# One semaphore for both tanh parts, fewer waits of VectorE on itself, its loop turned elsewhere, the last stage reordered

## The reference

```
def derivative(q, p, drive):                      # q, p: 8 x 1024
    dq = q - q**3/3 - p + drive + tanh(q) @ coupling.T + bias
    dp = EPSILON * (q + ALPHA - BETA*p)
# RK4: dq1..dq4 at q, q+DT/2*dq1, q+DT/2*dq2, q+DT*dq3; p alike
q = clip(q + DT/6*(dq1+2*dq2+2*dq3+dq4), -20, 20); p = clip(p + ..., -20, 20)
x[:, t, :] += q
```

## Time and profile before

| | us |
|---|---|
| median of 3 runs | 5836.68 |
| the profiled execution | 5833.99 |
| its span | 5832.2 |
| VectorE busy | 5405.9 (93%) |
| TensorE busy | 4466.0 (77%) |
| ScalarE busy | 2597.8 (45%) |
| granted TensorE clock, mean share of full speed | 0.995 |

### The profile page before, as it was taken

The page is one execution under the profiler, slowest core; times in us unless marked ns, Lnnn a source line. Parts: engine busy times, 40 slices in busy tenths (PEclk is TensorE's granted clock), DMA queues, the critical chain, the costliest instruction groups (busy, mean ns, idle before and its releaser), DMA issues.

```text
span 5832.2 us, 592464 instructions
## 1 busy us (share of the span) xinstructions
PE 4466.0 (77%) x263627; PEld 3814.6 (65%) x263627; DVE 5405.9 (93%) x31566; ACT 2597.8 (45%) x12040; POOL 5.7 (0%) x16
## 2 busy tenths in 40 slices
PE   7887777777777777777777777777777777777777
PEld 3446666666666666666666666666666666666666
DVE  5569999999999999999999999999999999999999
ACT  3334444444444444444444444444444444444444
POOL 0000000000000000000000000000000000000000
PEclk9999999999999999999999999999999999999999
DMA  5100000000000000000000000000000000000000
GB/s 214 46 16 0 0 7 0 7 0 7 0 0 7 0 7 0 7 0 0 7 0 7 0 7 0 0 7 0 7 0 7 0 0 7 0 7 0 7 0 7
DMA packets 11597, 57.06 MB, mean 10 GB/s; under 512 B 2616, under 2 KB 2616, under 8 KB 8512
## 3 DMA queue, kind: packets, MB, share of 16 engines
q1 hardware_dynamic: 11056, 55.84, 2.4%
q10 hardware_dynamic: 528, 1.05, 0.1%
HBM read 40.11 MB, written 16.78 MB: 10 GB/s over the span
## 4 chain that ended last, share of the span: by engine, by line
DVE 48%; PE 33%; issue 16%; ACT 1%; DMA 1%; DVEq 0%; SPq 0%; ACTq 0%
PE ps L633 29%; DVE xb L675 24%; DVE xb L835 10%; DVE tanh_parts L675 6%; DVE xb L858 2%; DVE xb L950 2%; DVE xb L959 2%; PE ps L522 1%; ACT xb L446 1%; PE ps L577 1%; PE ps L540 1%; PE ps L556 1%; PE ps L566 1%; DVE drive L675 1%; DVE xb L964 1%
## 5 line engine op out<-in xcount | busy, mean ns | idle before, releaser
L633 PE MATMUL ps<-coup,tanh_parts 128*16 128x96 f16 (+1 forms) x262272 | 4120.1, 219 | 1286.1 <-DVE tanh_parts L675 1271.8
L633 PEld LDWEIGHTS ps<-coup,tanh_parts 128*16 128x16 f16 x262272 | 3654.6, 89 | 1752.3 <-issue 933.0
L675 DVE SCALAR_TENSOR_TENSOR xb<-xb 128x64 f32<-128x64 f32 (+2 forms) x17412 | 2998.8, 209 | 17.6
L446 ACT ACTIVATE xb<-xb 128x24 f32<-128x24 f32 (+1 forms) x4098 | 940.0, 229 | 2758.7 <-DVE xb L675 2747.9
L835 DVE STREAM_TRANSPOSE xb<-ps 128x96 f32<-128x96 f32 (+1 forms) x4096 | 1291.3, 315 | 198.0 <-PE ps L633 67.5
L675 DVE SCALAR_TENSOR_TENSOR tanh_parts<-xb,tanh_parts 128x24 f16<-128x24 f32 (+1 forms) x4098 | 697.9, 170 | 32.1
L495 ACT ACTIVATE xb<-xb 128x64 f32<-128x64 f32 x2048 | 500.2, 244 | 109.3 <-DVE xb L964 109.3
L452 ACT ACTIVATE tanh_parts<-xb 128x24 f16<-128x24 f32 (+1 forms) x2050 | 470.5, 230 | 64.5
L858 DVE SCALAR_TENSOR_TENSOR xb<-xb 128x64 f32<-128x64 f32 x2049 | 452.9, 221 | 0.0
L464 ACT ACTIVATE tanh_parts<-xb 128x24 f16<-128x24 f32 (+1 forms) x2048 | 356.6, 221 | 32.2
L458 ACT ACTIVATE xb<-xb 128x64 f32<-128x64 f32 x1024 | 263.5, 257 | 0.0
(11 more groups left out here) (69 smaller groups left out, 712.6 us busy)
## 6 DMA issues: line engine op xcount, KB each, us to landing
xb<-in_x SPq DMA_DIRECT2D x8, 2048.0 KB, 8.0
drive<-in_x_pt SPq DMA_DIRECT2D x8, 2048.0 KB, 25.0
out_pt<-drive SPq DMA_DIRECT2D x16, 1024.0 KB, 4.5
drive<-in_coupling_t SPq DMA_DIRECT2D x8, 512.0 KB, 11.8
mask_v<-in_cond SPq DMA_DIRECT2D x8, 132.0 KB
probs<-in_wo ACTq DMA_DIRECT2D x1, 1024.0 KB, 6.2
w_qkv<-in_wq SPq DMA_DIRECT2D x1, 64.0 KB, 4.4
w_qkv<-in_wk SPq DMA_DIRECT2D x1, 64.0 KB, 5.3
```

The source lines that it names most:

```text
L446: nc.scalar.activation(cols(tanh_sb, CHUNKS[j]), cols(q, CHUNKS[j]), ACT.Tanh, scale=unit_of[1.0])\
L633: last = nc.tensor.matmul(product(s, j)[SQ * g:SQ * g + ROWS, :], tanh_parts[:, s % 2, k, :], coup[:, k, part, g, n0:n1, :].rearrange("p c ...
L675: return V.scalar_tensor_tensor(out=out, in0=a, scalar=factor, in1=c, op0=ALU.mult, op1=op1)
```

## The change

**Semaphores.** `first_ready` and `rest_ready` of a chunk become one, `parts_ready`, which ScalarE and VectorE both raise; TensorE waits for 2 per stage, once, where it waited for each. `base_ready`, `z_rest_ready`, `p_ready`, `drive_p_ready` go; `z_ready` and `side_ready` are raised once per stage by the instruction that makes z (or y, a sum, p) and waited for at most once. In `z_of_first` of stage 3 the wait on the drive is replaced by one on `square_ready`, which ScalarE raises when it has squared the clipped q.

**Order of stage 3.** `look_ahead` goes from right behind T0 to between `cubic_of` and `base_of`; `p_next` takes its place; `clip_p` goes from behind q of chunk 1 to ahead of T1; `drive_less_p` and `clip_q` change places. In stage 2 `trace` and `p_sum_q3` change places, with a wait on `q_next` for the latter.

**The loop.** `stage` is cut in two behind the REST of chunk 1, and the loop of VectorE turns there, in stage 0, rather than behind `base_of`.

```diff
-                            pe.wait_ge(first_ready[kj], now)
-                            pe.wait_ge(rest_ready[kj], now)
+                            pe.wait_ge(parts_ready[kj], parts)
...
             def q_of(s, j, now):
-                if j == 0:
-                    dve.wait_ge(base_ready, now)
                 dve.wait_ge(product_turned[j], now)
...
                 if s == 3:
-                    look_ahead(now_at, (now + 2 * STAGES) * (COLS // STAGES))
+                    p_next()
                 q_of(s, 0, now)
...
                 if s == 3:
-                    p_next()
+                    clip_p(now)
                 turn_product(s, 1, now)
                 rest_of(parity, 0, made)
                 q_of(s, 1, now)
...
                 if s == 2:
                     z_without_last(now)
-                    trace((now - 3) * (COLS // STAGES))
+                    p_sum_q3(made)
                 if s == 3:
-                    clip_p()
+                    drive_less_p(1 - now_at)
                     clip_q(made)
-                    drive_less_p(1 - now_at, now)
                 rest_of(parity, 1, made)
+                return made
+
+            def after_rest(s, now_at, made):
...
                     cubic_of(3, made)
-                    p_sum_q3()
+                    trace((made - 4) * (COLS // STAGES))
                     base_of(3, made)
                 if s == 3:
-                    z_of_first(now).then_inc(z_ready, STAGES)
+                    dve.wait_ge(square_ready, made)
+                    z_of_first()
                     g0_of()
-                    dve.wait_ge(z_ready, now)
-                    with_first_part(0, z_first_part, z)
+                    with_first_part(0, z_first_part, z, made)
                     cubic_of(0, made)
+                    look_ahead(now_at, (made - 1 + 2 * STAGES) * (COLS // STAGES))
                     base_of(0, made)
...
-            stage(0, 0, 1)
+            made = until_rest(0, 0, 1)
             with dve.Fori(2, 2 + STAGES * (STEPS - UNROLLED), STAGES * UNROLLED) as now:
-                for s, now_at in order:
+                after_rest(0, 0, now)
+                for s, now_at in between:
                     now = stage(s, now_at, now)
+                until_rest(0, 0, now)
```

More of the change, by code:

```diff
@@ L260, in build @@
         tanh_ready = [sem(f"tanh_ready{j}") for j in range(NCH)]
-        first_ready = [sem(f"first_ready{j}") for j in range(NCH)]
-        rest_ready = [sem(f"rest_ready{j}") for j in range(NCH)]
+        parts_ready = [sem(f"parts_ready{j}") for j in range(NCH)]
         start_ready = sem("start_ready")
@@ L646, in _ @@
             last.then_inc(start_done, 1)
-            with pe.Fori(1, 1 + STAGES * STEPS, PE_STAGES) as now:
+            with pe.Fori(PARTS, PARTS * (1 + STAGES * STEPS), PARTS * PE_STAGES) as parts:
                 for s in range(PE_STAGES):
@@ L663, in _ @@
                         if place == len(ORDER) // 2:
-                            after = pe.snap(now + 1)
-                    now = after
+                            after = pe.snap(parts + PARTS)
+                    parts = after
         @block.vector
@@ L851, in rest_of @@
                 axpy(tanh_part(parity, j, REST), by_block(tanh_sb, CHUNKS[j]), TANH_SCALE,
-                     tanh_part(1 - parity, j, FIRST), ALU.subtract).then_inc(rest_ready[j], 1)
+                     tanh_part(1 - parity, j, FIRST), ALU.subtract).then_inc(parts_ready[j], 1)
             def cubic_of(stage, made):
@@ L864, in base_of, with with_first_part, z_of_first @@
                 dve.wait_ge(cubic_ready, made)
-                axpy(base[:, :], cubic[:, :], -STEP[stage] / 3 if stage < 3 else CURVE, z_first_part[:, :]).then_inc(base_ready, 1)
-            def with_first_part(stage, out, z_of_stage):
+                axpy(base[:, :], cubic[:, :], -STEP[stage] / 3 if stage < 3 else CURVE, z_first_part[:, :])
+            def with_first_part(stage, out, z_of_stage, made):
+                dve.wait_ge(z_ready, made)
                 return axpy(all_blocks(out), first_sums(), STEP[stage], all_blocks(z_of_stage))
[L871 to L875, removed]
+            def z_of_first():
+                return axpy(z[:, :], drive_p[:, :], DT / 2, q_st[0][:, :]).then_inc(z_ready, 1)
             def z_of_second():
-                axpy(z2[:, :], g0[:, :], -DT / 2 * RISE, z[:, :])
+                axpy(z2[:, :], g0[:, :], -DT / 2 * RISE, z[:, :]).then_inc(z_ready, 1)
             def y_of():
-                axpy(y[:, :], drive_p[:, :], DT, q_st[0][:, :])
+                axpy(y[:, :], drive_p[:, :], DT, q_st[0][:, :]).then_inc(side_ready, 1)
             def y_less_g0():
@@ L888, in z_of_third @@
             def z_of_third():
-                axpy(z3[:, :], rise[:, :], -DT * RISE * G1[1], y_less[:, :])
+                axpy(z3[:, :], rise[:, :], -DT * RISE * G1[1], y_less[:, :]).then_inc(z_ready, 1)
             def rise_of_first():
@@ L933, in p_sum_g0 @@
             def p_sum_g0():
-                axpy(p_sum[0][:, :], g0[:, :], P_SUM[0] / P_ALL, q_st[0][:, :], ALU.subtract)
+                axpy(p_sum[0][:, :], g0[:, :], P_SUM[0] / P_ALL, q_st[0][:, :], ALU.subtract)\
+                 .then_inc(side_ready, 1)
             def p_sum_r1():
@@ L941, in p_sum_q2, with p_sum_q3, clip_p, drive_less_p @@
                 axpy(p_sum[2][:, :], q_st[2][:, :], P_SUM[2] / P_ALL, p_sum[1][:, :])
-            def p_sum_q3():
+            def p_sum_q3(made):
+                dve.wait_ge(q_next[NCH - 1], made)
                 axpy(p_sum[3][:, :], q_st[3][:, :], 1 / P_ALL, p_sum[2][:, :])
             def p_next():
[L947 to L951, removed]
+                axpy(p_raw[:, :], p_sum[3][:, :], DT / 6 * EPS * P_ALL, p_st[:, :]).then_inc(side_ready, 1)
+            def clip_p(now):
+                dve.wait_ge(side_ready, now)
+                V.tensor_scalar(p_st[:, :], p_raw[:, :], bounds[:, 2:3], bounds[:, 3:4], ALU.max, ALU.min)
             def look_ahead(into, at):
                 axpy(drive_b[into][:, :], drive_cols[:, bass.ds(at, COLS)], inv_unit[:, 0:1], bias_b[:, :])
[L957 to L960, removed]
+            def drive_less_p(now_at):
+                V.tensor_tensor(drive_p[:, :], drive_b[now_at][:, :], p_st[:, :], ALU.subtract)
             def clip_q(made):
@@ L983, in _, with until_rest @@
             last.then_inc(start_turned, 1)
+            dve.wait_ge(start_turned, 1)
+            with_first_part(0, z_first_part, z, 1).then_inc(setup, 1)
             dve.wait_ge(setup, 10)
-            dve.wait_ge(start_turned, 1)
-            with_first_part(0, z_first_part, z).then_inc(setup, 1)
-            dve.wait_ge(setup, 11)
             base_of(0, 1)
             g0_of()
-            def stage(s, now_at, now):
+            def until_rest(s, now_at, now):
                 following = (s + 1) % STAGES
@@ L1038, in stage @@
                 if s == 1:
-                    with_first_part(2, z_first_part, z3)
+                    with_first_part(2, z_first_part, z3, made)
                     cubic_of(2, made)
```

36 lines of the change are left out of this document (17 added, 19 removed).

## The result

The changed kernel takes 5695.42 us (median of 4 runs, 5694.53 to 5696.95) against 5836.88 of the kernel before (4 runs): a ratio of 0.9758, 95% interval 0.9741 to 0.9775. The forecast was 5762, with a range from 5715 to 5812.

The account below looks back on a forecast made before the run. Bound: a circle from TensorE to VectorE and back, neither engine alone. Two stages each at 2.51, 2.55, 2.74, one at 2.55 and one at 2.63 make 20.78 us against 21.07: 74 us less, 5762 us, range 5715 to 5812.

Parts of the forecast that it names:

- The circles: TensorE-VectorE loop, T1 (transpose of chunk 1) to T1: chunk 0 2.50 us; chunk 1 2.51 in stage 1, 2.55 in 0, 2.
- One semaphore per chunk: TensorE's first load after REST: gap 0.12 to 0.05 us, the gain cut to 0.06 and 0.02 by chunk 1.
- T0 to T1: VectorE's time between the two transposes: 0.62 to 0.58 us with q earlier, counting in stage 3 and at the turn.
- Stage 3: TensorE's 0.19 us stall goes, but z waits for the square until +1.27; stage from 2.76 to 2.74 us.
- rival C: In stage 3 the wait for the square doesn't bind: stage 2.55 us, 97 us less, 5665 us; chance 0.05.
- The look ahead: Between cubic and base in stage 3: holds VectorE 0.20 us, so base comes 0.34 after cubic.
- The turn: VectorE's loop turn behind REST of chunk 1: costs the same 0.48 us, not hidden; its stage 2.68 to 2.63 us.
- A: TensorE's merged wait gains nothing, the 0.12 us stays: 28 us gained in all, 5809 us; chance 0.15.
- B: VectorE's removed waits buy nothing, transpose to transpose stays 0.62 us: 31 us, 5793 us; chance 0.07.
- D: VectorE's loop turn costs more in its new place: at 0.68 us, 13 us slower, 5849 us; chance 0.07.

## Why the prediction was right in kind and wrong in size

**The circles.** Right: but for stage 3 and the turn, which VectorE sets, each stage is set by the way from T1 through REST or FIRST to TensorE and back, and chunk 1 is late next. Stages 0 and 2 stay 0.03 to 0.04 longer than stage 1, as forecast. In stage 2 the reason is the forecast one, FIRST of chunk 1 ends last. In stage 0 behind a stage 3 FIRST of chunk 0 is late as well: the first load comes 0.51 after T1 (3010.14 to 3010.65; 0.47 in stage 2) and waits for ScalarE, which the prediction didn't have. The two ways come out within 0.01 there, so the length was right partly by luck.

**One semaphore per chunk: the term that was mis-sized.** I took the gap from REST's end to the first load, 0.12 to 0.05, and kept 1.37 from load to T1, a number read where the load stood behind a separate wait. That number held 0.02 to 0.03 of the separate wait's cost as well: with one wait the first matmul starts with the load, not 0.03 behind it. Where TensorE stands still for chunk 1 and sets T1, in stage 3 of the kernel with the clips as before, 1.34 pass from load to T1 with one wait. The stages came out 0.02 to 0.03 shorter than forecast, five of them 0.12 a turn, 31 us. My bounds for this term (0.03 and 0.12) covered only the gap to the load, so they left the other part out of the range.

**T0 to T1: the other term.** I took 0.04 from 0.62 for the separate wait, from the 0.38 at which q of chunk 0 starts behind T0 and an axpy spacing of 0.14, read among axpys in a row. The 0.38 is a row of stage 3, where the look ahead stood between T0 and q and no axpy, and the first axpy behind T0 makes way sooner than 0.14: its successor starts 0.11 after it. In the changed kernel q starts 0.31 behind T0, the three between take 0.43, and T1 comes 0.54 or 0.55 behind T0. The wait was worth 0.07 to 0.08 and not 0.04. That is 0.03 to 0.04 in three stages a turn; by the table stage 3 and the turn are 0.11 a turn under the forecast, 29 us, with 0.01 from the chain of stage 3 in it. This term had no bounds at all. The two make 60 of the 67 us; I put the rest to rounding to 0.01 and the spread of the runs.

**Stage 3.** Right to 0.05: the stall of TensorE goes, and the wait for the square holds z at +1.27 as before. What the prediction did not say is that VectorE's own chain is as long as it was: the look ahead adds 0.08 to it and the shorter T0 to T1 takes 0.07 to 0.08 away, so stage 3 is 2.694 with the new order and 2.690 with the merge alone. The 0.07 under the old 2.764 is what TensorE's stall stood above that chain, and the merge alone gives it too. That the removal of the wait for the square sets TensorE free again (rival C's size, 97 us) was measured as 98.

**The look ahead.** Right: it holds VectorE 0.20 and lengthens the chain; base is 0.08 later and stage 3 0.07 longer, twice a turn.

**The turn.** Right: moved, not hidden. The stage is 0.02 under its forecast 2.63 by T0 to T1.

**Rivals.** A is refuted by the merge alone (the words give it six stages at 2.57, its sum of 20.96 has the right five), B by the wait for base put back, C by the 512 waits for the square and a stage 3 of 2.69, D by the 0.49 at the turn and by the loop of double length. C's price is that of the next change to this kernel.

## What to carry to other kernels

Where an engine waits for two things, ask which comes last and whether it has an instruction of its own: one semaphore for both takes 0.09 us from such a wait here, 0.05 to 0.09 from most stages of a chain of 2048, and that is 122 of the 141 us; the later one on the working instruction, with both kept, gave 55. When a stall is removed, look at what the same edit makes wait: here the time that the new order of stage 3 freed went into its new wait for ScalarE, and the look ahead took what the shorter T0 to T1 gave; 100 us more lay in waiting for the clip instead. A duration read behind a wait carries a part of that wait with it; give each such term its own bounds.

## What the runs showed of the hardware

A separate waiting instruction of TensorE costs more than the delay of the next load: the first matmul stands 0.15 behind the end of REST with it and 0.05 or 0.06 without. The load behind the waiting one comes 0.033 after it with the separate instruction and 0.003 without; why, the runs don't settle. On VectorE a separate waiting instruction ahead of q of chunk 0 makes T0 to T1 0.62 where it is 0.54 without. At the turn of VectorE's loop the next instruction starts 0.48 us behind the last in the old place, where 0.14 is usual, and 0.49 in the new one, where 0.12 is usual (3011.02 to 3011.14 in the changed kernel); it is 0.49 in the loop of double length too.
